# A landing wait in front of every second pair of gathers, in the second edge stage of a graph network kernel

## The reference

```python
# second layer's edge stage: sum of the source rows of each node's edges
summed = jax.ops.segment_sum(x[src], dst, num_segments=n)
deg = jax.ops.segment_sum(jnp.ones_like(src, dtype=x.dtype), dst, num_segments=n)
agg = summed / jnp.maximum(deg, 1.0)[:, None]
out = jnp.concatenate([x, agg], axis=-1) @ weight
out = out / jnp.linalg.norm(out, axis=-1, keepdims=True)
...
# its mixing stage: linear attention over 8 heads, then two matrix products with a gelu
k = _ln(k, kln_g, kln_b)
v = _ln(v, vln_g, vln_b)
kv = jnp.einsum('bhnd,bhne->bhde', k, v) / HW
out = jnp.einsum('bhnd,bhde->bhne', q, kv)
...
# its expert stage: 8 experts of three products each, for every node
h = jnp.einsum('bfd,edh->bfeh', x, W1) + b1
h = jax.nn.relu(_bn(h, g1, be1, m1, v1))
h = jnp.einsum('bfeh,ehk->bfek', h, W2) + b2
h = jax.nn.relu(_bn(h, g2, be2, m2, v2))
y = jnp.einsum('bfeh,ehd->bfed', h, Wo) + bo
return jnp.einsum('bfed,fe->bfd', y, w)
```

## Time and profile before

| | |
|---|---|
| median of 3 timed runs | 2891.04 us |
| span of the profiled execution | 2911.8 us |
| span less median | 20.8 us |
| PE busy | 2563.1 us (88%) |
| POOL busy | 1185.6 us (41%) |
| gathers of the second edge stage | 392, 974 ns each on POOL |
| mean granted TensorE clock | 0.918 of full |

### The profile page before, as it was taken

How to read it: one execution, slowest core, us unless ns; L and a number is a source line. 1 busy time by engine, 2 the same in 40 slices (tenths; PEclk the granted TensorE clock), 3 DMA queues, 4 the chain that set the end, 5 groups by cost and what they waited for, 6 DMA issues and landing times. The chain is left out here.

```text
span 2911.8 us, 47805 instructions
## 1 busy us (share of the span) xinstructions
PE 2563.1 (88%) x16831; PEld 2377.1 (82%) x16831; DVE 1693.7 (58%) x4350; ACT 1330.1 (46%) x2855; POOL 1185.6 (41%) x1326
## 2 busy tenths in 40 slices
PE   6788899899989998998995999549899999998998
PEld 6778898889888988885675888439898888898898
DVE  4566777677766776555666232355556444444665
ACT  3234565455545554445532122212245454444687
POOL 1223453345434543456840222366654455554100
PEclk9889999999999999998985899856889899999899
DMA  4211112111211120124214444332221232233011
GB/s 106 66 37 37 37 44 66 37 37 43 68 37 37 42 68 23 47 55 107 83 54 118 151 143 139 117 108 84 86 87 38 71 97 84 86 95 92 21 45 29
DMA packets 137166, 205.25 MB, mean 70 GB/s; under 512 B 35134, under 2 KB 98430, under 8 KB 136803
## 3 DMA queue, kind: packets, MB, share of 16 engines
q1 hardware_dynamic: 99842, 107.97, 12.4%
q0 software_dynamic: 37088, 94.23, 11.8%
HBM read 168.50 MB, written 33.62 MB: 69 GB/s over the span
## 5 line engine op out<-in xcount | busy, mean ns | idle before, releaser
L922 POOL DMA_INDIRECT gat<-table,srcT x400 | 412.8, 1032 | 359.0 <-DVE m L2640 259.4
L1066 POOL DMA_INDIRECT x_rows<-table,srcT x392 | 381.6, 974 | 306.4 <-PE pg L1834 146.7
L588 PE MATMUL pa<-w,act 128*125 128x256 f32 x2400 | 362.3, 289 | 12.4 <-DVE act L2399 11.9
L588 PE MATMUL pb<-hT,w 128*128 128x378 f32 (+1 forms) x1920 | 342.3, 315 | 10.9 <-ACT gf L1905 8.5
L588 PEld LDWEIGHTS pa<-w,act 128*125 128x125 f32 x2400 | 317.5, 189 | 17.3 <-DVE act L2399 16.5
L2154 ACT ACTIVATE gf<-pb,bne 128x378 f32<-128x378 f32 (+1 forms) x320 | 194.2, 607 | 252.7 <-PE pb L588 137.5
L588 PEld LDWEIGHTS pb<-hT,w 128*128 128x128 f32 x1920 | 291.7, 192 | 14.9 <-ACT gf L1905 6.4
L1905 ACT ACTIVATE gf<-pb,b1s 128x378 f32<-128x378 f32 (+1 forms) x320 | 165.9, 519 | 139.7 <-PE pb L588 93.8
L2399 DVE TENSOR_TENSOR act<-gf,act 128x378 fp32r<-128x378 f32 (+1 forms) x320 | 153.7, 483 | 102.6 <-ACT act L1908 66.1
L588 PE MATMUL pb<-act,fw 128*128 128x378 f32 (+1 forms) x960 | 169.7, 329 | 29.2 <-ACT gf L2154 28.7
L588 PEld LDWEIGHTS pb<-act,fw 128*128 128x128 f32 x960 | 152.6, 202 | 31.9 <-issue 31.9
(11 more groups left out here) (492 smaller groups left out, 5694.9 us busy)
## 6 DMA issues: line engine op xcount, KB each, us to landing
e<-in_L_ffn_W_dram SPq DMA_DIRECT2D x40, 512.0 KB, 4.6
spill<-m SPq DMA_DIRECT2D x80, 170.0 KB
msg<-spill SPq DMA_DIRECT2D x40, 340.0 KB, 2.9
yslots<-yo SPq DMA_DIRECT2D x64, 128.0 KB, 2.0
fraw<-in_L_ffn_W_dram SPq DMA_DIRECT2D x32, 256.0 KB
w1r<-in_L_mix_W_dram SPq DMA_DIRECT2D x7, 1024.0 KB, 4.9
gat<-table,srcT POOLq DMA_INDIRECT x400
x_rows<-table,srcT POOLq DMA_INDIRECT x392
```

The costliest lines, as they stand in the source:

```text
L588: mm = nc.tensor.matmul(ps, lhs(l), rhs(r), start=first and n == 0, stop=last and n == 2)
L922: pool.indirect_dma_start(out=gat[:, i % 2, c, :], out_offset=None, in_=table0, in_offset=bass.IndirectOffsetOnAxis(ap=srcT[:, i * GC + c: ...
L1066: pool.indirect_dma_start(out=x_rows[:, n % UB, c, :], out_offset=None, in_=table1, in_offset=bass.IndirectOffsetOnAxis(ap=srcT[:, at:at + ...
```

## The change

In `fetch_pairs`, before the two DMAs of every even pair but the first, POOL now waits until the rows of the pair before have landed: the `rw` semaphore of that pair's place has its full count. The count includes what an earlier use of the same semaphores added (for places 0 to 3). Odd pairs are issued as before. No other instruction is changed.

```diff
+        def pair_landed(n):
+
+            b = n % UB
+            return s[f"rw{b}"], 16 * UC * (n // UB + 1) + (len(range(b, NT, 4)) * 32 if b < 4 else 0)
+
         def fetch_pairs(pairs):
 
             for n in pairs:
                 if n >= UB:
                     pool.wait_ge(s["win_ps"], NPR + n - UB + 1)
+                if n and n % 2 == 0:
+                    pool.wait_ge(*pair_landed(n - 1))
                 for c in range(UC):
                     at = pair(n) * UC + c
                     pool.indirect_dma_start(out=x_rows[:, n % UB, c, :], out_offset=None, in_=table1,
```

## The result

| | before | after |
|---|---|---|
| time, us (median) | 2890.28 (2888.86 to 2899.61, 4 runs) | 2970.18 (2965.59 to 2978.17, 4 runs) |
| profiled span, us | 2911.8 | 2976.5 |

The change makes the kernel slower: the ratio of the times is 1.027, with a 95% interval of 1.0249 to 1.0291, some 80 us. The prediction was 2875 us, with a range up to 2925. The result lies beyond it, on the slower side.

What follows compares the result with a forecast made beforehand. PE was taken to set the pace, with gaps in stages 1 and 3 from late counts. Stage 3 -31.5, stage 1 +15 and stage 2 +1 gave -15.5 us from 2891.04: 2875 us, range 2835 to 2925.

Steps and rivals of the forecast that it cites:

- the price of one wait: POOL's added time per wait for its own landed gather: taken as 1.5 us, bounds 1.4 to 2.4 us.
- the prediction's own slope: Each 0.1 us on the wait moves the sum by 8.4 us, 5.9 in stage 3 and 2.5 in stage 1.
- rival 1: The landing costs more, so POOL's cycle binds stages 1 and 3; slower from 1.7 us per wait, up to 2951; chance 0.2.
- Stage 3: Second edge stage, first to last burst: POOL's cycle binds at 383 us instead of 414.5, a gain of 31.5 us.
- Stage 1: Windows 0 to 49: POOL's two pairs take 6.5 us, so 168 us in place of 152.8, 15 us more.
- the 5% that I added for slow spells: In stage 1, time lost to slow clock spells: raises 3.26 us a pair to 3.43.
- Stage 2: Half of its waits fall into gaps already there, so it loses only 1 us.
- late counts: Counts of other engines seen late until a run of over four gathers drains; on ACT 92.0 us in stage 3.
- PE's floor of 356 us: Stage 3's time if PE ran without stalls, 15.1 us per ten pairs' half, 23.5 such periods.
- With no run above four the late counts go: Cutting gather runs to four ends the late counts, so stage 3 gains 31.5 us.
- Rival 2: The stall is smaller in timed than in profiled runs: about 2896 us, at the extreme 2963; chance 0.12.
- Rivals 3 and 4: 3: half the waits hidden, -58 us, 2833, chance 0.16; 4: late counts stay with runs of four, +16, 2907, chance 0.12.

Runs made afterwards that it cites:

- e2_stages12_only: Against the kernel before: the wait stands only before the even pairs 2 to 74 (stages 1 and 2); 2936.04 us, ratio 1.0166.
- e4_every_pair: Against the kernel before: every pair waits for the landing of the pair ahead, 195 waits in place of the change's 97; 3190.51 us, ratio 1.0907.
- c2_change: The change, unchanged, run beside the kernel before where counts are late; 2982.33 us, ratio 1.0211.
- d3_change_again: The change again, run beside the kernel before where no counts are late; 2901.0 us, ratio 1.0541.
- set 4: Runs on one chip of the kernel before (traced), the change, and pauses before every even pair or stage 3's third pairs; before took 2921.4 us.
- set 2: Runs on one chip: wait or pause before stage 3's third pairs, a wait before every pair, half the rows; before took 2926.8 us.
- set 1: Runs on one chip: wait in some stages only, a cap on gathers not landed, gathers left out; before took 2892.7 us.
- Sets 2 and 5: Two groups of runs, each beside the kernel before (2926.8 and 2748.5 us); the latter has pauses of two and ten memsets and the change again.
- set 3: Runs on one chip with short pauses in place of the wait, at three choices of places; before took 2747.0 us.

## Why the prediction was wrong

**The step that failed is the price of one wait**, "I take 1.5 us". It measured 2.54 - 0.30 = 2.24 us, near the high end of its bounds (2.4). The landing itself was sized right: it is there 1.80 us after the issue's end, and PE goes on 0.04 us later. What I left out is what POOL needs from the landing to its next gather, which no row of DVE shows: 0.74 us. Of this 0.26 us also stand where the gather waits for one semaphore. The other 0.48 us come only where it waits for two. That is a comparison of places in the traces (0.26 us in all 12 places with one, in this trace and in those of `e2_stages12_only`, `e4_every_pair`, `c2_change` and `d3_change_again`; 0.74 in all other waits of these five), and no run took the second wait away. With a gap of 2.04 us, as with one semaphore, the price would be 1.74 us, and by the prediction's own slope the sum would be near nothing (an estimate: -15.5 + 8.4 x 2.4 = +5 us).

I had named the wake-up of POOL in rival 1 and gave it no number. That rival is what happened: it decides from 1.7 us, and at 2.24 us the prediction's slope gives -15.5 + 8.4 x 7.4 = +47 us in the profile.

**The rest up to +64.7.** Stage 3: POOL's cycle at the measured price is 20 x 1.255 + 5 x 2.24 = 36.3 us for ten pairs, 427 us for 117.5 pairs. The stage took 439.5. Of the other 13 us, 11 are waits in which the rows landed late: in 13 of the stage's 57 waits from pair 82 on the landing came over 2.1 us after the issue's end, once 4.24. The prediction had one size for all landings. What delays some of them stays open. PE's granted clock of 0.89 (0.95 before) and its 42.5 us of waits for rows go with this; POOL sets the pace. Stage 1: 49 x 7.28 / 2 = 178.4 us by the cycle alone, 178.3 measured. So the 5% that I added for slow spells was wrong there, since POOL's pace covers them. It hid 8 us of the error. Stage 2: +8.8 us and not +1. Its waits aren't hidden half. And 5.8 us come after the start of the last burst: 2.2 of them are that burst's own wait for its last rows, the rest I can't tell.

**What held.** The late counts of ACT went, from 92.0 to 4.1 us. PE's floor of 356 us in stage 3 was 354 without gathers and 352 to 356 in the sets without late counts, the change left out. The weight of one wait held too, by half the rows and by twice the waits.

**What was half right.** "With no run above four the late counts go" gives too simple a cause. With a break after the fourth gather 61.5 to 70.8 us stay, and yet the stage gains 45 us in set 4 (424.2 to 379.2), and 27 and 30 us in set 2 against the first measurement. There the late counts are shorter each, and PE's waits for ACT fall from 33.7 to 10.0 us (set 4). So it seems to matter how long each one is and whether PE is held by it, more than their sum on ACT; this is argued from the traces, and no run shows it. In the change they may have gone because POOL never issues more than four gathers in 7.3 us. That reading fits all runs (a cap on landings does nothing, a pause does some, a wait in every second pair does all), but no run proves it: the two that varied the pause's length fell where no counts are late.

**Rival 2** (the stall is smaller in timed runs) isn't why the change lost: in set 1 leaving out the gathers won 88.6 us in timed runs. But something near it came up that I hadn't thought of. The traces of three sets and of the first measurement have late counts, those of the other two sets have none. The change buys off a loss which isn't always there, and pays always. Rivals 3 and 4 are refuted: no wait was hidden, and the late counts went.

**A better version.** The short pause before the third pair of each run of three in stage 3 beats both kernels where counts are late (ratios 0.9878 and 0.9889), and pauses of two and ten memsets in its place are equal to before (0.9996, 0.9998 and 0.9998) where they aren't. The pause of five memsets in stage 3 alone ran only where counts are late.

## What to carry to other kernels

A wait is priced on the engine that waits, with the waits that its instruction already has. The same landing freed PE after 1.84 us and POOL's next gather after 2.53, and with one such wait in every two pairs that difference decided the sign. 0.48 us of it came only with a second semaphore.

Where a wait only serves to break up an unbroken issue, first look for the place that has slack. There, in 23 places of stage 3, the wait for a landing still won 1.0% and a short pause 1.1 to 1.2%, while the wait in every second pair lost 2.1 to 2.7%. And before a stall is bought off, see whether it is there in every set of runs.

## What the runs showed of the hardware

- The same kernel before took 2747 and 2748 us in two sets, and 2893, 2927 and 2921 in three. The traces of the two kinds of set differ in one kind of wait: "remote", over 90 us on ACT in stage 3 of the kernel before (first measurement and set 4) and more elsewhere in the slower kind, not one in all six traces of the other. Those six are of other kernels, since the kernel before was not traced there; the three with pauses of two or ten memsets in stage 3 time the same as it. Stage 3 takes 352 to 354 us in these three, and 403 to 424 in the slower kind for kernels that fetch it as before. Sets 2 and 5 name the same chip number and are of different kinds, so I can't say whether it is the chip or its condition.
- With all gathers after the first ten left out, 2804 us in set 1 is still above the 2747 us of set 3 with them, and its trace has late counts in the earlier stages (126 us of waits for "remote", none of them on ACT's `gf` of stage 3). So late counts aren't bound to the gathers of the second edge stage.
- From the end of a gather's issue to the last update of its semaphore: 1.80 us in the median, up to 4.24 in the trace after. From there to PE's next product it is 0.04 us. To POOL's next gather it is 0.26 us if it waits for one semaphore, 0.74 if it waits for two. With half the rows POOL's gap is 2.31 us instead of 2.54.
